# Decoder layer on one core: scan halves redistributed over the score slots, and the score stacks loaded by pairs of heads

## The chip, the cores and the metric

The kernel runs on one core of a Trainium2 chip. The metric is the device time of one execution in microseconds. Three executions of the kernel before took 1580.32, 1584.42 and 1585.39 us; their median is 1584.42 us. The profile is of a fourth execution.

## The reference

Four batches, each 512 rows of 512 values, go through one post-norm decoder layer of three blocks, each followed by a residual addition and a layer norm:

```python
x = layernorm(x + attention(x))          # 16 heads of 32, softmax, plus a small "splat" term
x = layernorm(x + ssm(ctx, z=x))         # in-projection, conv of 4 taps, silu, selective scan of 16 states
x = layernorm(x + ffn(x))                # ternary weights, silu(gate) * up, rms norm, down projection
```

Attention is softmax(q k' / sqrt(32)) v for each head; in the splat term the attention weights come from distances of q and k to 8 points per head. The scan block works on the context, not on x, until its last product (y * silu(z)), so it can run beside the attention. For each of 512 channels and 16 states it computes

```python
state = state * exp(delta * A[n]) + (delta * u) * B[n]     # over 512 time steps
y    += state * C[n]
```

## The kernel before, in words

**Order of the work.** All four batches are unrolled by hand: for batch b (0 to 3) an attention phase and an FFN phase follow one another, and each engine (PE, ACT, DVE, POOL, and SP as the queue of most DMAs) has its own program of the phase, joined by semaphores. An engine does its own list strictly in order.

**Scan halves.** The scan of a batch is cut into 32 halves (n, a): state n of 16, channel half a of 2 (256 of the 512 channels). Half number g = 2n + a costs:
- ACT: `exp_dA` (L571), two activations of 512 steps into the buffer dA[a]; it waits until scan g - 2 is done.
- DVE: `scan_half` (L858), a product (L866), the scan itself (L874) and a product (L877). It waits for row n of B and C (`BC`, loaded on SP, L333), for dA and, in a ring of three buffers ST, for the accumulation of half g - 3.
- POOL: a DMA (L471) that adds the result to YA in memory, issued one half later.

SP loads row n + 1 of B and C when it comes to half (n, 0) in its own list (`load_next_bc`, L354), after the product of half (n - 1, 1).

**Where the halves go.** `fill_halves` puts some between the projections that open the attention phase (the fill stage), `tile_halves` puts the first 16 halves of batches 1 to 3 into the FFN phase of the batch before, and `slot_halves(j, first)` (L261) puts the rest into the four score slots. It returns, for slot j, one list for each of the four steps kt (called c on DVE). It is read by SP, POOL, ACT and DVE alike. In batch 0 (`first`) slots 0 to 3 have 3, 3, 4 and 3 halves and three more follow behind the slots. In batches 1 to 3 the slots have:

| slot | step 0 | step 1 | step 2 | step 3 |
|---|---|---|---|---|
| 0 | - | - | - | (11,1) (12,0) |
| 1 | - | (12,1) | - | (13,0) (13,1) |
| 2 | - | (14,0) | - | (14,1) (15,0) |
| 3 | - | - | - | (15,1) |

**A score slot.** Slot j handles the four heads 4j to 4j + 3. Queries and keys, split into a high and a low part of reduced precision, are stored to memory (`qk_parts`) and come back as stacks QS[j % 2] and KS[j % 2] of 96 rows for four heads; `load_stack` (L339) issues six DMAs of 256 KB for them, all on one semaphore. Stacks 0 and 1 are loaded in the fill stage, behind the stores of the units u = 2 and u = 3, and the stores of the next units stand behind them in SP's list; stacks 2 and 3 are loaded when the scores of slot 0 and of slot 1 are done (step 3, ahead of that step's `load_next_bc`).
 - The row maxima of slot j + 1 are found during slot j: PE computes 16 tiles (`max_scores`, L1249, matmul L1264), four for each head, in two banks, and DVE reduces each (L930). Tile m goes to head m // 4; tile m waits for the maximum of tile m - 2. In slots 1 and 2 the steps 0, 1 and 2 take 4, 6 and 6 tiles. PE waits for the stack before tile 0 only.
 - The maxima go through PE and ACT into the bias row of the stack (`bias_row`, L622).
 - For each step kt PE computes the scores of four heads in two pairs (L1373), ACT takes their exponentials (L709), and PE multiplies those of the step before with the values and with ones (L1281).
 - After the slot ACT makes the inverse of the denominators (`inverse_start`, L642, its last instruction L647), and DVE normalises (`normalise`, L932, L936 to L940).

**The last slot.** In slot 3 there are no maxima left to find. It has the end of the splat term (`splat_normalise` L964, the numerators L1405 on PE, `add_splat` L983 on DVE, which frees their banks and on which the numerator two groups later waits), and, but for batch 3, the start of the next batch's scan block: transposes of the context (L1223), the in-projections (L1232), their copies on ACT (L584, L590, L591) and the convolution on DVE (`conv`, L879, three instructions at L885 for each of four channel tiles). Because two banks are needed for that, scores use one pair of banks (4 and 5) in slot 3 of batches 0 to 2: PE's next pair of scores waits for ACT's exponentials of the pair before. In batch 3 all four banks are there. On ACT the `exp_dA` of a step stand ahead of that step's exponentials (L693 ahead of L697). On DVE, step 3 has `add_splat(2)`, the convolution of three channel tiles, and half (15,1); then come normalise(3), add_splat(3), the fourth convolution, and the first layer norm. PE's output projection (L1416) does three of four groups of heads for two row tiles after the last values, and all the rest after add_splat(3).

## Time and profile before

| | us |
|---|---|
| median of 3 executions | 1584.42 |
| profiled execution, its own time | 1582.52 |
| its span, first to last instruction | 1580.8 |
| PE busy | 1226.0 |
| DVE busy | 1246.4 |
| ACT busy | 759.4 |
| POOL busy | 213.3 |

The attention phases, from the first maximum of slot 0 to the end of the output projection, take in batches 1 to 3 some 145 to 170 us each. The timeline of an engine gives the start of a group of equal instructions, their time together, and in brackets how long the engine had been idle before it and on whom it had waited. An x8 beside a matmul counts passes.

### The profile page before, as it was taken

The page shows a single profiled execution, that of the slowest core. Times are in us where ns is not written, and L with a number is a line of the kernel's source. Part 1 is how long each engine was busy: PE and PEld are TensorE (multiplying, and loading weights), DVE is VectorE, ACT ScalarE, POOL GpSimd, SP SyncE. Part 2 cuts the span into 40 slices and gives each one's busy share as a digit, 9 for nine tenths or more (in the row PEclk, how much of TensorE's full clock was granted, in tenths as well). Part 3 has the DMA queues.
Part 4 walks back from the last instruction along what each step waited for, and adds up shares of the span by engine and source line. Part 5 has one row for each costly group of instructions (what it writes and reads, how often), then busy time and mean ns, then how long its engine had stood idle before and what let it go on. Part 6 is the DMA issues. An engine that isn't in the chain of part 4 may idle for free.

```text
span 1580.8 us, 14027 instructions
## 1 busy us (share of the span) xinstructions
PE 1226.0 (78%) x4570; PEld 570.7 (36%) x4570; DVE 1246.4 (79%) x1485; ACT 759.4 (48%) x1110; POOL 213.3 (13%) x247
## 2 busy tenths in 40 slices
PE   4664746778688897778888886878888887788796
PEld 3332212223244442323344532323344532333453
DVE  5867978777989996885889995785889995877534
ACT  6775425435366632545466642545466633534232
POOL 1000221000111132100111132000111132001000
PEclk8756878779789898879889997789889998779798
DMA  6843794555439868451249776451248777462131
GB/s 196 272 161 109 168 222 118 115 118 111 101 82 234 211 171 215 94 140 34 62 118 238 184 194 178 94 144 30 62 120 237 183 182 182 92 150 41 36 105 66
DMA packets 112151, 220.15 MB, mean 139 GB/s; under 512 B 14048, under 2 KB 24800, under 8 KB 112080
## 3 DMA queue, kind: packets, MB, share of 16 engines
q1 hardware_dynamic: 92704, 151.24, 32.9%
q0 software_dynamic: 18432, 67.12, 21.9%
q10 hardware_dynamic: 944, 0.92, 0.2%
q8 instruction: 36, 0.59, 0.1%
q14 instruction: 35, 0.29, 0.1%
HBM read 122.37 MB, written 29.62 MB: 96 GB/s over the span
## 4 chain that ended last, share of the span: by engine, by line
DVE 39%; PE 28%; issue 10%; DMA 6%; ACT 3%; SPq 1%; POOL 1%; DVEq 0%; ACTq 0%; POOLq 0%
DVE ST L874 14%; DVE ST L866 6%; PE ps L1463 5%; PE ps L1264 5%; DVE MX L930 5%; PE ps L1281 4%; DMA KS<-qk_parts 3%; PE ps L1416 2%; DVE RD L1077 2%; DVE ST L877 2%; DVE QAK L1092 2%; PE ps L1373 2%; PE ps L1432 2%; PE ps L1345 2%; DVE BST L910 1%
## 5 line engine op out<-in xcount | busy, mean ns | idle before, releaser
L874 DVE TENSOR_TENSOR_SCAN ST<-dA,ST 128x1024 f32<-128x1024 f32 x128 | 311.8, 2436 | 8.8 <-ACT dA L577 6.0
L930 DVE TENSOR_REDUCE MX<-ps 128x1 f32<-128x512 f32 x256 | 165.3, 686 | 117.5 <-PE ps L1264 117.4
L1463 PE MATMUL ps<-V,GU 128*128 128x512 f16 x1024 | 243.3, 394 | 5.6 <-DVE V L1059 5.6
L471 POOL DMA_DIRECT2D YA<-ST x128 | 111.0, 867 | 1012.2 <-DVE ST L877 953.9
L1264 PE MATMUL ps<-KS,QS 96*128 96x512 f32 x256 | 134.1, 599 | 116.0 <-DVE MX L930 53.0
L577 ACT ACTIVATE dA<-DL,Aneg 128x511 f32<-128x511 f32 x256 | 168.9, 713 | 82.9 <-DVE ST L874 82.6
L709 ACT ACTIVATE PT<-ps 128x1024 f32<-128x1024 f32 x128 | 126.4, 1021 | 124.4 <-PE ps L1373 123.7
L1432 PE MATMUL ps<-WP,QS 128*128 128x512 f32 x512 | 145.8, 429 | 28.3 <-DMA WP<-proj_tiles 20.6
L877 DVE TENSOR_TENSOR ST<-ST,BC 128x1024 f32<-128x1024 f32 x128 | 159.4, 1246 | 4.4
L866 DVE TENSOR_TENSOR ST<-DU,BC 128x1024 f32<-128x1024 f32 x128 | 156.8, 1225 | 6.7 <-DMA BC<-bc_rows 6.5
L1463 PEld LDWEIGHTS ps<-V,GU 128*128 128x128 bf16 x1024 | 98.2, 101 | 139.2 <-issue 32.1
L1264 PEld LDWEIGHTS ps<-KS,QS 96*128 96x128 f32 x256 | 58.1, 243 | 212.5 <-DVE MX L930 109.9
L1345 PE MATMUL ps<-XA,W 128*128 128x512 f32 x256 | 121.9, 623 | 0.0
L1432 PEld LDWEIGHTS ps<-WP,QS 128*128 128x128 f32 x512 | 98.7, 198 | 63.8 <-issue 24.6
L1373 PE MATMUL ps<-QS,KS 97*128 97x512 f32 x256 | 95.3, 472 | 20.2 <-ACT PT L709 18.6
L757 ACT CAST QS<-QAK 128x512 fp32r<-128x512 f32 x64 | 39.5, 618 | 121.4 <-DVE QAK L1092 121.4
L1281 PE MATMUL ps<-PT,V 128*32 128x512 f32 x512 | 86.6, 755 | 9.5 <-ACT PT L709 9.5
L1092 DVE TENSOR_TENSOR QAK<-QAK,ps 128x512 f32<-128x512 f32 x64 | 43.7, 683 | 51.9 <-PE ps L1463 51.9
L1281 PE MATMUL ps<-PT,ones 128*32 128x512 f32 x512 | 79.1, 694 | 0.0
L1345 PEld LDWEIGHTS ps<-XA,W 128*128 128x128 f32 x256 | 51.0, 202 | 61.6 <-issue 59.1
L1373 PEld LDWEIGHTS ps<-QS,KS 97*128 97x128 f32 x256 | 50.4, 215 | 57.3 <-ACT PT L709 26.0
L1416 PE MATMUL ps<-W,XA 128*128 128x512 f32 x128 | 61.9, 642 | 10.8 <-DVE XA L987 10.8
(230 smaller groups left out, 1606.9 us busy)
## 6 DMA issues: line engine op xcount, KB each, us to landing
YA<-ST POOLq DMA_DIRECT2D x128, 512.0 KB, 7.3
BC<-bc_rows SPq DMA_DIRECT2D x64, 512.0 KB, 6.3
qk_parts<-PT SPq DMA_DIRECT2D x64, 256.0 KB, 6.3
GU<-gu_tiles SPq DMA_DIRECT2D x64, 256.0 KB, 9.1
WP<-proj_tiles SPq DMA_DIRECT2D x64, 256.0 KB, 6.7
QS<-qk_parts SPq DMA_DIRECT2D x48, 256.0 KB, 5.3
KS<-qk_parts SPq DMA_DIRECT2D x48, 256.0 KB, 5.9
ST<-in_L_ffn_w_gate_up_dram SPq DMA_DIRECT2D x16, 256.0 KB, 3.5
```

The costliest lines, as they stand in the source:

```text
L577: last = nc.scalar.activation(dA[:, a, e, 1:S], DL[:, 2 * a + e, 1:S], ACT.Exp, scale=Aneg[:, 2 * a + e, n:n + 1])
L709: nc.scalar.activation(PT[:, kt % 2, 2 * p:2 * p + 2, :], ps[:, bank:bank + 2, :], ACT.Exp, scale=SCALE).then_inc(s_exp, 1)
L866: nc.vector.tensor_tensor(ST[:, ring(bb, n, a), :, :], DU[:, 2 * a:2 * a + 2, :], BC[:, n % 2, 0:1, :].broadcast_to((P, 2, S)), ALU.mult). ...
L874: nc.vector.tensor_tensor_scan(flat, dA[:, a, :, :].rearrange("p e s -> p (e s)"), flat, 0.0, ALU.mult, ALU.add).then_inc(s_scan, 1)
L877: nc.vector.tensor_tensor(st, st, BC[:, n % 2, 1:2, :].broadcast_to((P, 2, S)), ALU.mult).then_inc(s_prod, 1)
L930: nc.vector.tensor_reduce(MX[:, j % 2, qt, h:h + 1], ps[:, n % 2, :], AX_X, ALU.max).then_inc(s_mx, 1)
L1264: mm(ps[:, n % 2, :], QS[i][0:3 * D, h, qt * P:(qt + 1) * P], KS[i][0:3 * D, h, :], start=True, stop=True).then_inc(s_xs, 1)
L1281: last = mm(ps[D * h:D * h + D, bank, :], w, PT[:, kt % 2, h, :], start=(kt == 0), stop=(kt == KT - 1), tile_position=(0, D * h))
L1345: last = mm(bank, W[:, z, k, j * P:(j + 1) * P], XA[:, k, :], start=(k == 0), stop=(k == KT - 1))
L1373: last = mm(ps[:, score_bank(b, j, h), :], KS[i][0:3 * D + 1, h, kt * P:(kt + 1) * P], QS[i][0:3 * D + 1, h, :], start=True, stop=True)
L1432: last = mm(ps[:, 4 + r, :], HL[:, 2 * z + t % 2, r * P:(r + 1) * P], WP[:, t % 2, :], start=(t == 0 and z == 0), stop=(t == NT - 1 and z ...
L1463: last = mm(ps[:, f % F_RING, :], GU[:, t % GU_RING, k, m * P:(m + 1) * P], XHL[:, z, k, :], start=(k == 0 and z == 0), stop=(k == KT - 1 ...
```

## The change

`slot_halves` returns other lists. In batches 1 to 3 slots 0, 1 and 2 have two halves each, both in step 3, and slot 3 has three: (14,1) and (15,0) in step 1, (15,1) in step 2. In batch 0 slots 0 to 2 stay, and slot 3 has its same three halves as two in step 1 and one in step 2, none in step 3. On DVE the convolution of the first two channel tiles moves from step 3 of slot 3 to step 2, behind add_splat(1) and ahead of that step's half. `load_stack` issues twelve DMAs of 128 KB in place of six of 256 KB: first six for heads 0 and 1, then six for heads 2 and 3, each pair with a semaphore of its own. PE waits for the first pair before tile 0 and for the second before tile 8.

```diff
-        s_stack = [sem(f"s_stack{i}") for i in range(2)]
+        s_stack = [[sem(f"s_stack{i}_{pair}") for pair in range(HG // 2)] for i in range(2)]
...
             rest = todo(first)[len(places(first)):]
-            upto = [len(rest) * share // 14 for share in (0, 3, 6, 9, 12, 14)] if first else (0, 2, 5, 8, 9, 9)
+            upto = [len(rest) * share // 14 for share in (0, 3, 6, 9, 12, 14)] if first else (0, 2, 4, 6, 9, 9)
             mine = rest[upto[j]:upto[j + 1]]
             if j == NG:
                 return [mine]
             if j < NG - 1:
                 third = len(mine) // 3
                 return [[], mine[:third], [], mine[third:]]
-            return [mine[len(mine) * c // KT:len(mine) * (c + 1) // KT] for c in range(KT)]
+            return [[], mine[:2], mine[2:3], mine[3:]]
...
-                for r, (zq, zk) in enumerate(((0, 0), (0, 1), (1, 0))):
-                    for z, dst, part in ((0, QS[i], zq), (1, KS[i], zk)):
-                        src = qk_parts[b, z, part, P * j:P * j + P, :].rearrange("(h p) s -> p h s", p=D)
-                        sp.dma_start(dst[D * r:D * r + D, :, :].bitcast(F32), src).then_inc(s_stack[i], 16)
+                for pair in range(HG // 2):
+                    first_row = P * j + 2 * D * pair
+                    for r, (zq, zk) in enumerate(((0, 0), (0, 1), (1, 0))):
+                        for z, dst, part in ((0, QS[i], zq), (1, KS[i], zk)):
+                            src = qk_parts[b, z, part, first_row:first_row + 2 * D, :].rearrange("(h p) s -> p h s", p=D)
+                            sp.dma_start(dst[D * r:D * r + D, 2 * pair:2 * pair + 2, :].bitcast(F32), src).then_inc(s_stack[i][pair], 16)
...
                             if c == 2:
                                 add_splat(b, 0)
                                 add_splat(b, 1)
+                                if not last:
+                                    conv(b + 1, 0)
+                                    conv(b + 1, 1)
                             if c == 3:
                                 add_splat(b, 2)
                                 if not last:
-                                    for e in range(KT - 1):
-                                        conv(b + 1, e)
+                                    conv(b + 1, 2)
...
             def max_scores(b, j, lo, hi):
                 i = j % 2
-                if lo == 0 and hi > 0:
-                    pe.wait_ge(s_stack[i], 96 * (2 * b + j // 2 + 1))
                 if lo == 0 and hi > 0 and j == 0:
                     pe.wait_ge(s_hi, 2 * NG * b + 4)
                 for m in range(lo, hi):
                     n = 16 * j + m
                     h, qt = m // KT, m % KT
+                    if m % (2 * KT) == 0:
+                        pe.wait_ge(s_stack[i][h // 2], 96 * (2 * b + j // 2 + 1))
```

## Rows read from the trace of the kernel before

**Rows 1.** The page, busy time of each engine.

```profile
PE 1226.0 (78%) x4570; PEld 570.7 (36%) x4570; DVE 1246.4 (79%) x1485; ACT 759.4 (48%) x1110; POOL 213.3 (13%) x247
```

**Rows 2.** The waits: who waited for whom, us in total, times, longest.

```profile
PE ps L1264 <- DMA KS<-qk_parts: 52.7, 8, 11.5
```

**Rows 3.** Timeline of DVE, slot 1 of batch 2.

```profile
1025.74 1.22 DVE L866 TENSOR_TENSOR ST<-DU,BC 128x1024 f32<-128x1024 f32 x1
...
1030.46 2.56 DVE L930 TENSOR_REDUCE MX<-ps 128x1 f32<-128x512 f32 x4
1034.83 1.29 DVE L930 TENSOR_REDUCE MX<-ps 128x1 f32<-128x512 f32 x2 [1.80 <-PE ps L1264]
```

**Rows 4.** Timeline of PE, slot 1 of batch 2.

```profile
1031.20 1.09 PE L1264 MATMUL ps<-KS,QS 96*128 96x512 f32 x2 [3.38 <-DVE MX L930]
```

**Rows 5.** Timeline of DVE, slot 3 of batch 2.

```profile
1082.74 0.69 DVE L972 SCALAR_TENSOR_TENSOR QAK<-X 128x512 f32<-128x512 f32 x1
1092.06 1.61 DVE L987 SCALAR_TENSOR_TENSOR XA<-ps,par,XA 128x512 f32<-128x512 f32 x2 [8.63 <-PE ps L1405]
1101.57 0.75 DVE L987 SCALAR_TENSOR_TENSOR XA<-ps,par,XA 128x512 f32<-128x512 f32 x1 [7.91 <-PE ps L1405]
1102.24 7.57 DVE L885 SCALAR_TENSOR_TENSOR W<-W,convw 128x511 f32<-128x511 f32 x9
...
1114.45 0.68 DVE L936 TENSOR_TENSOR X<-ps,RD 128x512 f32<-128x512 f32 x1
```

**Rows 6.** Timeline of ACT, slots 2 and 3 of batch 2.

```profile
1061.13 2.54 ACT L577 ACTIVATE dA<-DL,Aneg 128x511 f32<-128x511 f32 x4
...
1109.10 0.63 ACT L647 ACTIVATE RD<-RD 128x512 f32<-128x512 f32 x1
```

**Rows 7.** Timeline of PE, slot 3 of batch 2 and the output projection.

```profile
1083.26 0.97 PE L1373 MATMUL ps<-QS,KS 97*128 97x512 f32 x2 [2.04 <-ACT PT L709]
...
1108.33 5.42 PE L1416 MATMUL ps<-W,XA 128*128 128x512 f32 x12
1117.36 10.55 PE L1416 MATMUL ps<-W,XA 128*128 128x512 f32 x20 [3.61 <-DVE XA L987]
```

**Rows 8.** Timelines of DVE (first two) and PE, slot 3 of batch 3.

```profile
1432.74 0.69 DVE L972 SCALAR_TENSOR_TENSOR QAK<-X 128x512 f32<-128x512 f32 x1
...
1439.41 0.75 DVE L987 SCALAR_TENSOR_TENSOR XA<-ps,par,XA 128x512 f32<-128x512 f32 x1 [3.08 <-PE ps L1405]
...
1444.59 14.00 PE L1416 MATMUL ps<-W,XA 128*128 128x512 f32 x32
```

**Rows 9.** Stack 2 of batch 2: first and last issue on SP, then us to landing.

```profile
1004.94 0.32 SPq L352 DMA_DIRECT2D QS<-qk_parts  x1
...
1007.45 0.43 SPq L352 DMA_DIRECT2D KS<-qk_parts  x1
...
QS<-qk_parts SPq DMA_DIRECT2D x1, 256.0 KB, 3.1
...
KS<-qk_parts SPq DMA_DIRECT2D x1, 256.0 KB, 7.0
```

**Rows 10.** Timeline of DVE: first maxima behind stack 0, batches 1 to 3.

```profile
608.61 1.29 DVE L930 TENSOR_REDUCE MX<-ps 128x1 f32<-128x512 f32 x2 [2.62 <-PE ps L1264]
...
961.62 1.29 DVE L930 TENSOR_REDUCE MX<-ps 128x1 f32<-128x512 f32 x2 [5.04 <-PE ps L1264]
...
1314.69 1.29 DVE L930 TENSOR_REDUCE MX<-ps 128x1 f32<-128x512 f32 x2 [2.76 <-PE ps L1264]
```

**Rows 11.** The same behind stack 2, batches 0, 2 and 3.

```profile
288.75 1.29 DVE L930 TENSOR_REDUCE MX<-ps 128x1 f32<-128x512 f32 x2 [3.81 <-PE ps L1264]
...
1015.01 1.29 DVE L930 TENSOR_REDUCE MX<-ps 128x1 f32<-128x512 f32 x2 [2.25 <-PE ps L1264]
...
1365.31 1.29 DVE L930 TENSOR_REDUCE MX<-ps 128x1 f32<-128x512 f32 x2 [3.04 <-PE ps L1264]
```

**Rows 12.** Timeline of DVE, fill stage of batch 0.

```profile
221.54 1.23 DVE L866 TENSOR_TENSOR ST<-DU,BC 128x1024 f32<-128x1024 f32 x1 [6.53 <-DMA BC<-bc_rows]
```

## Prediction

> **What bounds the kernel now.** I read the page first, then the waits, then the timelines of DVE, PE, ACT and SP over the attention phases. The page shows no single bound: PE and DVE are each busy for 78 to 79% of the span [rows 1], so what counts is which of them waits for which, stage by stage. The waits say that PE stood still eight times, 52.7 us in all, before its first maximum tile because a stack had not landed [rows 2]. The timelines then show three patterns that repeat in the batches.
>
> First, slots 1 and 2 are bound by DVE. After the sixth tile of step 1 DVE does a scan half from 1025.74 to 1030.5, and PE, with two banks only, waits 3.38 us for the next maximum [rows 3, 4].
>
> Second, slot 3 is bound by PE and ACT handing each other one pair of score banks: PE waits 2.04 us for exponentials [rows 7], while DVE is idle for 8.63 and 7.91 us [rows 5]. The slot's end is bound by DVE again: nine convolutions and a half run from 1102.24 to 1114.45, although the inverse was ready at 1109.73 [rows 5, 6], and PE's output projection stands still for 3.61 us for them [rows 7].
>
> Third, DVE itself has nothing to do while a stack lands: 2.62, 5.04 and 2.76 us in the fill stage [rows 10], 3.81, 2.25 and 3.04 us at the start of slot 1 [rows 11], and batch 1 has the same 3.0 us there. Batch 0 waits in its fill stage for a row of B and C instead [rows 12].
>
> **Term 1: one half fewer in slots 1 and 2, batches 1 to 3 (six places).** A half is product, scan, product: 1030.46 - 1025.74 = 4.72 us of DVE. That is the upper bound of one place. Tiles 10 to 15 now end at 1036.12, that is 10.4 us after step 1's last tile, whose maximum ended at 1025.8 [rows 3]. Without the half, they take their 5.7 us from row 1030.46 to 1036.12, plus about 1.0 us, since PE must make the scores of its step ahead of tile 10 and no longer does so behind a half. That leaves 6.7 us and a gain of 3.7 us. The lower bound is PE's wait alone, 3.4 us [rows 4]. Everything behind (transposed maxima, scores, the two halves of step 3) keeps its distance. ACT's exp_dA for step 3 wait for scans two halves back, which are done a slot earlier. The row of B and C for a moved half is asked for one slot or more ahead of its use. Six times 3.7: **-22.2 us**.
>
> **Term 2: three halves and the split convolution in slot 3.** For DVE the new work fits: from 1083.43 the halves of step 1 take 2 x 4.72 us and end at 1092.9, against a numerator that came at 1092.06 [rows 5]. The price is on ACT, where the exp_dA stand ahead of the exponentials. Two of them are 2.54 us [rows 6], and PE's next pair of scores waits for just these exponentials [rows 7]; so everything behind in slot 3 comes 2.5 us later. The exp_dA of step 2 lies in ACT's own wait for scores and replaces the one of step 3: nothing, or 0.4 us if that cover is gone. Six convolutions (6 x 0.84 = 5.0 us) and the third half (4.7 us) then lie in DVE's second idle time, 7.9 us, and spill by under 2 us into the wait for the inverse.
> - Batches 1 and 2: the inverse comes at 1109.73 + 2.5 = 1112.3, and normalise and add_splat(3), 2.9 us, end at 1115.2. PE's first twelve projection passes end at 1113.75 + 2.5 = 1116.3, so PE is late next, not DVE: 1117.36 - 1116.3 = 1.1 us gained. The twenty passes behind the idle time took 0.53 us each, against 0.45 in the twelve ahead of it [rows 7] and 0.44 in batch 3, where none was idle [rows 8]: 20 x 0.09 = 1.8 us more. Together 2.8 us, twice. Bounds: a loss of 2.5 us if the longer wait at the slot's start slows PE as well; a gain of 3.6 + 1.8 us if ACT's delay were hidden.
> - Batch 0: one exp_dA more in step 1, 1.3 us. The wait of normalise behind the inverse, 1114.45 - 1109.73 = 4.7 us in batch 2 and alike there, becomes zero, and DVE's three halves behind the slots keep DVE the bound: 4.7 - 1.3 = 3.4 us gained.
> - Batch 3 has no next batch: PE has neither transposes nor in-projections, and DVE little idle time in this slot. From 1433.43 the two halves end at 1442.9; add_splat(0) and (1) come behind them, PE's third and fourth numerator (in order, ahead of the scores of step 3) wait for them until 1444.5, so that add_splat(2) has its numerator some 0.9 us later, at 1445.4, and not at 1439.4 [rows 8]. All of PE's list behind it moves by that. A loss of 6.0 us; bounds 5 and 9.5 (all of two halves).
>
> Sum of term 2: 2 x 2.8 + 3.4 - 6.0 = **-3.0 us**.
>
> **Term 3: stacks by pairs.** The six DMAs of stack 2 land from 1004.94 + 3.1 = 1008.0 to 1007.45 + 7.0 = 1014.45 [rows 9]: one each 1.28 us, in order. With half the bytes in each, six land one each 0.64 us from 1007.4 on: the first pair is there at 1010.6, 3.8 us earlier, and the issue of the sixth, at 1007.45, allows that. What DVE gains is the smaller of its wait and 3.8 us: 3.8 + 3.0 + 2.25 + 3.0 = 12.1 us at slot 1 [rows 11], and 2.6 + 3.8 + 2.8 = 9.2 us in the fill stage [rows 10]. In batch 0's fill stage DVE waits for B and C, which stands behind the stack in the queue [rows 12]: no gain. At slot 2 DVE is busy when stack 3 lands: nothing. Half-size DMAs are nowhere in this trace. The bounds of a DMA are 0.64 us (by bytes) and 1.28 us (by count); I take the first, since the DMAs land as evenly as a stream of bytes would. At 1.28 us the term is zero or, with what is queued behind, a loss (below).
>
> Six more issues of 0.43 to 0.47 us [rows 9] hold SP for 2.8 us per stack. Behind them stand stores of queries and keys, and B and C; all of these wait for the backlog of the stack's bytes anyway (the last stack DMA lands 7.0 us after its issue), so this costs nothing while the backlog is longer than 2.8 us. Were that cover gone, ACT's next unit in each fill stage would be late, up to 2.8 us in four batches. I put down a loss of 1.5 us in all. The second pair is wanted at tile 8, about 9 us behind tile 0 at slot 1, and lands no later than 3 us after the old stack. Term 3: **-19.8 us**.
>
> By the Trainium skill, page "DMA: Bandwidth & Descriptors", section "Rules for kernel authors", splitting a transfer into disjoint parts is not worth it, since both parts run on the same 16 engines and serialize, and DMAs should be large. What the rows show is that they do serialize, and that is what the early wait uses. By the Trainium skill's table of sizes (same page, section "Bandwidth"), an estimate for 128 KB is nearer 1 us than 0.64, so the first pair would gain 1.5 to 2 us rather than 3.8, and term 3 would be about half.
>
> **Sum.** -22.2 - 3.0 - 19.8 = -45.0 us. From the profiled execution's 1582.5 that is 1537.5. The median of the runs lies 1.9 us above that execution: **1539 us**.
>
> **The rivals.**
> - *The split loses its rate.* A half-size DMA takes as long as a whole one up to the point where the first pair lands as late as the stack did. For it: no such DMA in the trace. Against it: even landings. Term 3 is near zero: 1539 + 19.8 = 1559 us. Half-way, at 0.96 us each, 1549. The Trainium skill's rule above is this case.
> - *Slot 3 takes back more.* ACT's 2.5 us are paid, and PE runs slower behind the longer waits, so the projection's 1.8 us don't come: batches 1 and 2 lose 2.5 us each, batch 0 gains nothing, batch 3 pays 9.5 us. Term 2 becomes +14.5 in place of -3.0: 1556 us. For it: PE's 0.53 us passes. Against it: DVE's idle 16.5 us in two waits.
> - *Slower.* Each half-size DMA costs the full 1.28 us of the queue. Then a stack takes 7.7 us longer and what is queued behind it in the fill stage comes 7.7 us later: B and C in batch 0, where the 6.53 us [rows 12] become 14, and the stores on which ACT's next unit waits in the other three. That is 31 us on top of 1559: 1590 us. It decides from a spacing of about 1.2 us; at 1.0 us, the backlog costs less than half of that and the change still wins by term 1.
> - The change does what it says: the lists are fixed when the program is built.
>
> **How the numbers follow.** Forecast 0.68; the split loses its rate 0.13; slot 3 takes back more 0.15; slower 0.04. About 0.3% is what a measurement of this kernel can tell from no change: 4.8 us. All but the last lie beyond it: faster 0.96, same 0.01, slower 0.03. The range: below, term 1 at its upper bound (6 x 1.0 us more), both of batches 1 and 2 at theirs (2 x 2.6) and the 5.04 us wait gone entirely, 1.2: 1539 - 12.4, and some for PE's passes in the slots: 1524. Above it takes in slot 3's rival and the half-way case of the split, to 1557; left out are the full loss of the split and the slower case.
>
> **What would show it.** Slots 1 and 2: no L866 between the sixth and seventh maximum, and the maxima of step 2 ending 3.7 us earlier. Slot 3: DVE's waits before L987 nearly gone, ACT with four L577 ahead of step 1's exponentials, L936 directly behind L647, no wait before the twenty passes of L1416; in batch 3 a wait of PE for L987. Stacks: landings 0.64 us apart, DVE's waits of rows 10 and 11 near zero. Landings more than 1 us apart, or a new wait of ACT for qk_parts, would make term 3 wrong; a DVE wait in step 2 as long as the half was would make term 1 wrong.

## The result, and the profile after

The changed kernel takes **1520.3 us** (median of 4 runs, 1517.1 to 1522.4) against 1584.2 us before (4 runs beside it): a ratio of 0.9599, with a 95% interval of 0.9574 to 0.9624. That is 63.9 us less where 45 were forecast, and it lies 4 us below the range. The sign and the likeliest case were right; the size was not, and most of what follows asks where the other 19 us come from.

The page after, its first line and the busy times; and from the waits the three that matter (engine, line, who is waited for: us in total, how often, the longest). Lines 930, 1264, 1373, 987 and 936 of before are 932, 1268, 1377, 989 and 938 here.

```profile
span 1516.6 us, 14134 instructions
...
PE 1194.1 (79%) x4565; PEld 560.5 (37%) x4570; DVE 1245.1 (82%) x1485; ACT 759.7 (50%) x1110; POOL 214.6 (14%) x247
```

```profile
DVE MX L932 <- PE ps L1268: 84.0, 73, 3.8
...
PE ps L1377 <- ACT PT L711: 25.6, 14, 4.5
...
PE ps L1268 <- DMA KS<-qk_parts: 20.9, 4, 7.8
```

DVE does the same work as before, to 1.3 us [rows 1], in a shorter span. PE's wait for the stacks fell from 52.7 us [rows 2] to 20.9. But PE's *busy* time fell by 32 us too, although the two kernels make the same matmuls. No term of the prediction had anything of that kind. The mean granted clock of PE rose from 0.848 to 0.869 of full speed.

By stages, differences after minus before in the profiled executions (starts of instructions, read from the timelines; "fill" runs from the start of the span, or from PE's first feed-forward matmul of the batch ahead, L1463 and now L1467, to DVE's first maximum of the batch; slots 0 and 1 end at normalise(0) and normalise(1), slot 2 at the last instruction of `splat_normalise`, the last column at PE's first feed-forward matmul):

| batch | fill | slot 0 | slot 1 | slot 2 | slot 3 and projection |
|---|---|---|---|---|---|
| 0 | +0.2 | -4.0 | -0.1 | -5.0 | -3.1 |
| 1 | -1.4 | -3.2 | -4.5 | -6.5 | -1.5 |
| 2 | -6.0 | -6.4 | -4.2 | -6.3 | -1.8 |
| 3 | -3.4 | -3.6 | -4.6 | -5.6 | +7.1 |
| sum | -10.5 | -17.1 | -13.3 | -23.4 | +0.8 |
| forecast | -7.7 | -12.1 | -11.1 | -11.1 | -3.0 |

The start of slot 1, with its stack wait, counts in the column of slot 0, because normalise(0) stands behind it. The largest miss is slot 2: 12 us.

**Slot 1.** DVE's timeline of the changed kernel, batch 2 (start, us, engine, line, [idle before <- on whom]):

```profile
986.04 2.58 DVE L932 TENSOR_REDUCE MX<-ps 128x1 f32<-128x512 f32 x4 [1.55 <-PE ps L1268]
989.35 1.29 DVE L932 TENSOR_REDUCE MX<-ps 128x1 f32<-128x512 f32 x2 [0.73 <-PE ps L1268]
990.55 1.22 DVE L868 TENSOR_TENSOR ST<-DU,BC 128x1024 f32<-128x1024 f32 x1
```

The half is gone. In its place there are two short waits, 1.55 + 0.73 us, where the old slot had one of 1.80 [rows 3]: of the half's 4.7 us 0.5 were paid back, not the 1.0 I had put in.

**Slot 2.** The same stretch, tiles 8 to 15: first the kernel before, then the changed one.

```profile
1057.38 1.29 DVE L930 TENSOR_REDUCE MX<-ps 128x1 f32<-128x512 f32 x2 [0.96 <-PE ps L1264]
1058.59 1.22 DVE L866 TENSOR_TENSOR ST<-DU,BC 128x1024 f32<-128x1024 f32 x1
...
1063.31 1.28 DVE L930 TENSOR_REDUCE MX<-ps 128x1 f32<-128x512 f32 x2
1064.88 1.29 DVE L930 TENSOR_REDUCE MX<-ps 128x1 f32<-128x512 f32 x2 [0.29 <-PE ps L1264]
1068.07 1.29 DVE L930 TENSOR_REDUCE MX<-ps 128x1 f32<-128x512 f32 x2 [1.90 <-PE ps L1264]
```

```profile
1011.19 1.29 DVE L932 TENSOR_REDUCE MX<-ps 128x1 f32<-128x512 f32 x2 [1.77 <-PE ps L1268]
1013.69 2.58 DVE L932 TENSOR_REDUCE MX<-ps 128x1 f32<-128x512 f32 x4 [1.21 <-PE ps L1268]
1016.99 1.29 DVE L932 TENSOR_REDUCE MX<-ps 128x1 f32<-128x512 f32 x2 [0.72 <-PE ps L1268]
```

From the end of the first two maxima to the end of the last: 1069.36 - 1058.67 = 10.7 us before, 1018.28 - 1012.48 = 5.8 after. The waits are 0.29 + 1.90 before and 1.21 + 0.72 after, 0.26 us *less*: here the whole half, 4.7 us, was gain, and 0.2 more.

**Slot 3, batch 2.** ACT, PE and DVE of the changed kernel, one timeline each.

```profile
1030.36 2.56 ACT L579 ACTIVATE dA<-DL,Aneg 128x511 f32<-128x511 f32 x4
```

```profile
1033.88 1.22 PE L1377 MATMUL ps<-QS,KS 97*128 97x512 f32 x2 [4.47 <-ACT PT L711]
1035.03 1.94 PE L1285 MATMUL ps<-PT,V 128*32 128x512 f32 x8
1036.74 1.93 PE L1285 MATMUL ps<-PT,ones 128*32 128x512 f32 x8
1038.61 4.00 PE L1236 MATMUL ps<-QAK,inT 128*128 128x512 f32 x8
...
1059.84 14.00 PE L1420 MATMUL ps<-W,XA 128*128 128x512 f32 x32
```

```profile
1043.57 1.61 DVE L989 SCALAR_TENSOR_TENSOR XA<-ps,par,XA 128x512 f32<-128x512 f32 x2 [2.45 <-PE ps L1409]
...
1061.27 0.69 DVE L938 TENSOR_TENSOR X<-ps,RD 128x512 f32<-128x512 f32 x1 [3.42 <-ACT RD L649]
```

The pattern is the forecast one: two `exp_dA` of two activations each (the x4) ahead of the exponentials, PE's wait 4.47 us in place of 2.04 [rows 7] (2.4 more, 2.5 forecast), DVE's idle 16.5 us [rows 5] down to 2.45 before L989, the normalise behind the inverse, and 32 projection passes in one run at 0.44 us each. What I had not counted are the next PE rows. Behind the wait the two groups of eight take 1.94 and 1.93 us and L1236 takes 4.00, where later in the slot the same groups take 1.07, 1.04 and 3.70. The granted clock was at its lower level, 1.2 GHz (0.50 from 1034 to 1038 us, and 0.50 in the same stretch of batch 1). Before, behind the 2.04 us, the clock was low too (0.57 from 1083 to 1087 us) but came back sooner: scores, both groups and the in-projection took 0.97 + 1.93 + 1.59 + 3.70 = 8.2 us, now 1.22 + 1.94 + 1.93 + 4.00 = 9.1.

**Batch 3, slot 3.** PE, then DVE:

```profile
1373.01 3.03 PE L1409 MATMUL ps<-QAK 128*128 128x512 f32 x4 [4.56 <-DVE XA L989]
```

```profile
1382.46 0.69 DVE L938 TENSOR_TENSOR X<-ps,RD 128x512 f32<-128x512 f32 x1 [3.56 <-ACT RD L649]
```

As forecast, PE waits for a numerator that stands behind two halves: 7.1 us lost, 6.0 forecast.

**The stacks.** Issues of stack 2 in batch 1 on SP, the first, sixth and last of twelve; then from the view of DMA issues how long the sixth and the last took to land (us at the line's end):

```profile
634.76 0.32 SPq L354 DMA_DIRECT2D QS<-qk_parts  x1
...
637.32 0.43 SPq L354 DMA_DIRECT2D KS<-qk_parts  x1
...
640.63 1.39 SPq L354 DMA_DIRECT2D KS<-qk_parts  x1
```

```profile
KS<-qk_parts SPq DMA_DIRECT2D x1, 128.0 KB, 3.1
...
KS<-qk_parts SPq DMA_DIRECT2D x1, 128.0 KB, 5.8
```

The first pair is complete 637.32 + 3.1 - 634.76 = 5.7 us after the first issue: the forecast, 1010.6 - 1004.94. The second is complete 11.7 us after the first issue, some 2 us later than the whole stack before (9.5 us in [rows 9]; 9.9 for this stack in batch 1). The first eight halves land 0.4 to 1.1 us apart, 0.6 on average, where their issues stand 0.5 apart on average; the last four land 2.0, 1.2, 0.6 and 0.9 us apart.

### The profile page after: what moved, and what is told of

It reads as the page before. It is cut to its first block, busy times and chain, and to the rows that moved or that the text cites. A ratio compares the mean times of both kernels' runs of the same rounds, so it can differ in the third digit from the quotient of the medians.

```text
span 1516.6 us, 14134 instructions
## 1 busy us (share of the span) xinstructions
PE 1194.1 (79%) x4565; PEld 560.5 (37%) x4570; DVE 1245.1 (82%) x1485; ACT 759.7 (50%) x1110; POOL 214.6 (14%) x247
## 4 chain that ended last, share of the span: by engine, by line
DVE 39%; PE 30%; issue 10%; ACT 5%; DMA 4%; POOL 1%; SPq 1%; DVEq 0%; ACTq 0%; POOLq 0%
DVE ST L876 14%; DVE ST L868 6%; PE ps L1467 5%; PE ps L1285 5%; DVE MX L932 5%; PE ps L1268 4%; PE ps L1420 3%; PE ps L1349 2%; PE ps L1436 2%; DVE ST L879 2%; PE ps L1377 2%; DVE RD L1081 2%; DVE QAK L1096 2%; DMA qk_parts<-PT 2%; PE ps L1236 1%
## 5 line engine op out<-in xcount | busy, mean ns | idle before, releaser
L1467 PE MATMUL ps<-V,GU 128*128 128x512 f16 x1024 | 240.3, 390 | 5.6 <-DVE V L1063 5.6
L1268 PE MATMUL ps<-KS,QS 96*128 96x512 f32 x256 | 127.6, 560 | 74.1 <-DVE MX L932 42.3
L1467 PEld LDWEIGHTS ps<-V,GU 128*128 128x128 bf16 x1024 | 97.6, 100 | 136.5 <-issue 27.3
L1268 PEld LDWEIGHTS ps<-KS,QS 96*128 96x128 f32 x256 | 53.6, 223 | 164.7 <-DVE MX L932 95.1
L1285 PE MATMUL ps<-PT,V 128*32 128x512 f32 x512 | 81.1, 710 | 11.4 <-ACT PT L711 10.4
L1285 PE MATMUL ps<-PT,ones 128*32 128x512 f32 x512 | 74.6, 658 | 0.0
```

The lines of the kernel that those rows point to most:

```text
L1268: mm(ps[:, n % 2, :], QS[i][0:3 * D, h, qt * P:(qt + 1) * P], KS[i][0:3 * D, h, :], start=True, stop=True).then_inc(s_xs, 1)
L1285: last = mm(ps[D * h:D * h + D, bank, :], w, PT[:, kt % 2, h, :], start=(kt == 0), stop=(kt == KT - 1), tile_position=(0, D * h))
L1467: last = mm(ps[:, f % F_RING, :], GU[:, t % GU_RING, k, m * P:(m + 1) * P], XHL[:, z, k, :], start=(k == 0 and z == 0), stop=(k == KT - 1 ...
```

## What the rival theories were

*Theory C (the clock).* Each of these waits costs PE more than its length: the granted clock falls during it and what follows runs at half speed. Earlier stacks and fewer halves take these falls away; this is what the sum left out. *Rival W.* The waits are everything, and the sum was wrong because waits were sized too small (above all "the smaller of its wait and 3.8"). Windows of the timelines show what they argue about, around the start of slot 2 in batch 0: first before, then after. The columns are stretch, its length, busy us (and instructions) of PE, PEld, DVE, ACT and POOL, then the granted clock, DMA share, GB/s.

```profile
321.00:325.00 4.00, 1.15 (x4) 0.36 (x3) 1.43 (x2) 0.81 (x2) 0.00 (x0) 1.00 1.07 270
325.00:329.00 4.00, 3.45 (x9) 2.18 (x9) 2.77 (x5) 0.62 (x1) 0.00 (x0) 0.60 0.96 278
329.00:333.00 4.00, 4.00 (x14) 1.39 (x13) 2.38 (x4) 1.43 (x2) 0.00 (x0) 0.54 0.03 9
```

```profile
320.00:324.00 4.00, 3.72 (x18) 1.71 (x18) 3.98 (x7) 2.05 (x2) 0.00 (x0) 1.00 1.03 249
324.00:328.00 4.00, 3.78 (x24) 1.51 (x16) 3.23 (x5) 1.12 (x2) 0.00 (x0) 1.00 0.18 37
```

Before, PE waited for stack 3 while DVE had nothing to do either, and behind the wait PE's clock was 0.60, then 0.54 (the 1.2 GHz level is 0.50). After, it stayed at 1.00. In the prediction this wait stood as "DVE is busy when stack 3 lands: nothing". Two cautions go with these windows. The wait of before is longer here than this load needs: stack 3 took 11.6 us from its first issue to its last landing in this execution, and 9.8 in e2 below, which loads it whole too; there DVE waited 0.60 us in place of 2.56. And the windows are one execution of each kernel; e1 below shows the clock falling at this place with the stack early.

## The experiments

The variants were measured in three groups, each with runs of the kernel before beside it (medians 1581.2 for e1 to e4, 1581.2 for e7 to e10 and 1581.9 us for the others). A gain in us is one minus the ratio, times that median, unless medians are named. A ratio's interval is 0.0016 to 0.004 to either side, mostly 0.0025 or some 4 us; a difference of two ratios has an interval of some 5 to 6 us. By stages means one profiled execution of each kernel against one of before.

### The two parts alone

e1: the kernel before, with `load_stack`, `s_stack` and the waits of the change and nothing else of it.

```diff
-    for r, (zq, zk) in enumerate(...):  # six DMAs of 256 KB, one semaphore
+    for pair in range(HG // 2):         # twelve DMAs of 128 KB, one semaphore for each pair
...
+                    if m % (2 * KT) == 0:
+                        pe.wait_ge(s_stack[i][h // 2], 96 * (2 * b + j // 2 + 1))
```

> The kernel before with the stacks loaded by pairs, lists and convolution as before. Theory (PE's granted clock: a stall for a stack costs its own time and then a stretch in which PE runs at the lower level, so that removing the stall gains more than the stall, and stack 3 counts too): about 37 us faster than before, 1547 us, with slot 2 of batch 0 some 4 us shorter though nothing in it is moved. Rival 1 (the stalls are worth their length only, as predicted): 20 to 23 us, 1562 us. Rival 2 (the extra gain comes from the moved halves): 20 us here, and more than 40 us in the kernel with the lists alone.

Measured: 1551.1 us, ratio 0.9808 (0.9786 to 0.983): **-30.3 us**, where term 3 said -19.8: between the 20 to 23 us of one expectation and the 37 of the other.

e2: the changed kernel with stacks loaded as before, so lists of halves and convolution alone.

```diff
-        s_stack = [[sem(f"s_stack{i}_{pair}") for pair in range(HG // 2)] for i in range(2)]
+        s_stack = [sem(f"s_stack{i}") for i in range(2)]
```

> The kernel after with the stacks loaded whole, as before. Theory: 22 to 28 us faster than before (4.3 us for each of six places in slots 1 and 2, nothing to 3 us in slot 3), 1558 us. Rival 1: 25 us as predicted, 1559 us. Rival 2: over 40 us, 1543 us.

Measured: 1553.2 us, 0.9828 (0.9802 to 0.9855): **-27.2 us**, where terms 1 and 2 said -25.2. So the larger part of the miss is in term 3. The two ratios multiply to 0.9639 against 0.9599 for both together, 6 us with an uncertainty as large: whether the parts help each other stays open.

By stages e1 has -11.2 in the fill, -13.0 in slot 0, +0.4, -4.0 in slot 2, +0.6. e2 has -1.5, +1.0, -11.9, -19.7, +0.4. Of e2's slot 2, 16.8 us are in batches 1 to 3 and 2.9 in batch 0, whose list is unchanged there: in that slot this trace of before is itself at the slow end. So e1's 4.0 us in slot 2 are not the early stack's as they stand: 3.1 of them are in batch 0, where e2 has 2.9 with the stack late. In e1 the clock fell there all the same, with DVE's wait down to 0.59 us:

```profile
324.00:328.00 4.00, 4.00 (x14) 1.51 (x13) 2.58 (x4) 1.93 (x2) 0.00 (x0) 0.50 0.71 175
```

### The split without its early wait

e3: e1 with both pairs awaited before tile 0.

```diff
-                    if m % (2 * KT) == 0:
-                        pe.wait_ge(s_stack[i][h // 2], 96 * (2 * b + j // 2 + 1))
+                    if m == 0:
+                        for pair in range(HG // 2):
+                            pe.wait_ge(s_stack[i][pair], 96 * (2 * b + j // 2 + 1))
```

> The kernel before with twelve half-size DMAs per stack, but PE waits for both pairs ahead of tile 0. Tells whether the split itself costs or gives queue time. If half-size DMAs go by their bytes: within 3 us of before (1584 us). If each costs as much as a whole one: 25 to 31 us slower. If the split itself is what gains: faster by over 10 us.

Measured: 1602.7 us, 1.0131 (1.0091 to 1.0171): **21 us slower** than before, and between the two costs that were expected (within 3 us, or 25 to 31). The split costs something, and all of e1's gain is the early wait: 51 us lie between the two. The first and last issue of stack 3 in batch 1, the last one's landing, and what DVE then waited:

```profile
692.00 0.30 SPq L354 DMA_DIRECT2D QS<-qk_parts  x1
...
699.81 0.43 SPq L354 DMA_DIRECT2D KS<-qk_parts  x1
```

```profile
KS<-qk_parts SPq DMA_DIRECT2D x1, 128.0 KB, 5.9
```

```profile
706.75 1.29 DVE L932 TENSOR_REDUCE MX<-ps 128x1 f32<-128x512 f32 x2 [5.06 <-PE ps L1267]
```

The stack is complete 13.7 us after its first issue (10.3 before), and DVE's wait is 5.06 us where it was 1.07.

### The clock, with dummy matmuls

e4: before, with dummy matmuls of 128 x 256 in front of the waits for stacks 2 and 3 (six and three; the trace shows each as two passes). The waits stay, each stack's now directly ahead of its tile 0; PE is busy during them.

```diff
+                    if m == 0:
+                        for _ in range((0, 0, 6, 3)[j]):
+                            mm(ps[:, 0, 0:H // 2], W[:, 3, 0, 0:P], W[:, 3, 1, 0:H // 2], start=True, stop=True)
+                        pe.wait_ge(s_stack[i], 96 * (2 * b + j // 2 + 1))
```

> The kernel before, with PE doing matmuls that nobody reads (6 units of 256 columns ahead of tile 0 of stack 2, 3 ahead of tile 0 of stack 3, into the bank that tile 0 then overwrites) while it waits for the stack; all waits stay. Theory (clock): PE stays at its upper level behind the wait, and the first eight tiles of slots 1 and 2 take 7.2 us in place of 9.2: 5 to 12 us faster than before, 1575 us. Rival 1 (length of the stall only): no faster, 0 to 3 us slower.

Measured: 1571.1 us, 0.9938 (0.9914 to 0.9963): **-9.8 us** from matmuls that compute nothing. The window at the start of slot 2 in batch 0, and DVE there:

```profile
322.00:326.00 4.00, 3.26 (x12) 1.58 (x10) 3.71 (x6) 1.10 (x2) 0.00 (x0) 1.00 1.07 249
```

```profile
322.29 5.16 DVE L930 TENSOR_REDUCE MX<-ps 128x1 f32<-128x512 f32 x8 [1.89 <-PE ps L1266]
```

The wait for the stack is still there (1.89 us), but the eight maxima behind it run back to back, 5.2 us, at clock 1.00. Before, behind a wait of 2.56 us, they took from 325.35 to 331.80, 6.5 us, with three more waits among them, and the next two came 1.45 us later, where they come after 0.7 in e4. That is theory C's mechanism, with the stack no earlier. By stages slot 2 is 7.7 us shorter, 3.2 in batch 0 (where e2 has 2.9 with no dummies) and 1.9, 1.5 and 1.1 in the others; the profiled execution is the fastest of the nine, 6.5 us below their median.

e5: the same with 14 dummies, in front of stack 0 alone ((14, 0, 0, 0) in the line above).

> Before, with 14 dummy matmuls on TensorE in front of the wait for stack 0, which the 4.7 to 8 us wait of the next batch's first tile otherwise leaves idle. If what follows the stack waits is slow also because the granted clock has fallen during them, the tiles behind the wait get cheaper in the fill and in the first score slot: 1 to 2 us a batch, 3 to 8 us in all (time near 1576). If the clock plays no part there: nothing, or 1 to 3 us more, because the dummies end after the stack has landed.

Measured: 0.9998 (0.9981 to 1.0014): **nothing** in the whole, but not nothing in the trace. In batches 2 and 3 slot 0 is 4.5 and 3.4 us shorter while the fill keeps its length to 0.8 us. In batch 0 it is 8.1 us longer. One late window of slot 0 in batch 3, before and in e5 (DVE's wait for the maxima in it was 5.46 us before and 3.82 in e5):

```profile
1334.00:1339.00 5.00, 4.45 (x15) 1.15 (x11) 1.04 (x2) 1.50 (x4) 0.05 (x1) 0.78 0.05 18
```

```profile
1335.00:1340.00 5.00, 3.90 (x12) 1.92 (x12) 4.24 (x7) 4.16 (x7) 3.34 (x3) 1.00 0.01 3
```

And half of what batch 0 of e5 lost, in PE's timeline; before, this wait was 3.13 us:

```profile
296.47 1.19 PE L1266 MATMUL ps<-KS,QS 96*128 96x512 f32 x2 [6.98 <-DMA KS<-qk_parts]
```

The clock and slot 0's length go together in this trace too, but my expectation that it would show in the time fell. e5 also moves the waits for all stacks as e4 does, so that move is not what made e4 faster. Stack 2 of batch 0 landed later here; whether the dummies caused that or it varies between executions was not settled. Batch 0's slot 0 differs by -0.7 to +3.4 us in e1 and e2.

Slot 0's clock also varies with nothing changed. In batch 1 the kernel of e10 (below) runs the same instructions as the changed kernel, and in its trace slot 0 is 3.6 us longer: the clock was 1.00 there in the changed kernel, and in e10

```profile
624.00:629.00 5.00, 4.64 (x12) 3.04 (x12) 3.56 (x7) 3.14 (x5) 3.11 (x3) 0.61 0.30 58
```

and a group of eight took 1.94 us in place of 1.07. A difference of this size in one slot of one trace does not show what an edit did.

e11: the *changed* kernel with dummies in front of four of its waits.

```diff
+                    if j == 0 and m == 0:   # 8 dummies, stack 0
+                    if j == 2 and m == 2:   # 3 dummies, behind a wait for s_exp
...
+                                if one_pair and kt == 1 and p == 1:   # 8 dummies, last slot's second score pair
...
+                                pe.wait_ge(s_br, NG * b + 3)          # and 3 dummies, in slot 2
```

> The changed kernel with dummy matmuls in front of four of its waits: 8 ahead of the first tile of stack 0, 3 ahead of tile 2 of slot 1, 3 ahead of the normalise wait of slot 2, 8 ahead of the second score pair of step 1 in the last slot of batches 0 to 2. The theory (a wait also costs the clock of the matmuls behind it) says that the change has taken away part of these falls, and what is left is worth 5 to 10 us: near 1512. The rival (the clock is a remainder, the waits themselves are everything): within 3 us of the changed kernel, and slower where a dummy ends after what it waits for.

Measured: 1507.4 us, 0.9537 (0.9518 to 0.9556). Against the changed kernel's ratio, 0.0062 or **9.8 us less** (by some 5 us to either side), at the upper end of what was expected; the mean clock is 0.890. The place where it comes from is mostly the last slot: -5.3, -5.4 and -3.9 us in batches 0 to 2, where the change alone has -3.1, -1.5 and -1.8. PE there in batch 1, first the changed kernel, then e11:

```profile
702.79 1.22 PE L1377 MATMUL ps<-QS,KS 97*128 97x512 f32 x2 [4.47 <-ACT PT L711]
703.94 1.94 PE L1285 MATMUL ps<-PT,V 128*32 128x512 f32 x8
```

```profile
701.38 0.73 PE L1387 MATMUL ps<-QS,KS 97*128 97x512 f32 x2 [1.02 <-ACT PT L711]
702.04 1.06 PE L1292 MATMUL ps<-PT,V 128*32 128x512 f32 x8
```

### The last slot

e7: the changed kernel with the three convolutions together again in step 3.

```diff
-                                if not last:
-                                    conv(b + 1, 0)
-                                    conv(b + 1, 1)
...
-                                    conv(b + 1, 2)
+                                    for e in range(KT - 1):
+                                        conv(b + 1, e)
```

> The kernel after with nine convolution instructions in step 3 of the last slot, none in step 2, as before. Theory: the end of the slot is set by PE and ACT now, and DVE's step 3 has 3.4 us of idle time behind it in batches 0 to 2, so the split is worth 0 to 1 us per batch: 0 to 3 us slower than after. Rival (DVE still sets the end of the slot): 5.0 us per batch, 15 us slower.

Measured: 1520.3 us, 0.9622 (0.9591 to 0.9653), with slot 3 within 0.2 us of the changed kernel's in every batch. Splitting the convolution brings nothing that shows: the normalise waits for ACT's inverse in both.

e8: the changed kernel, but batch 3 with the old upper bounds (0, 2, 5, 8, 9, 9) and its one half of slot 3 in step 3.

```diff
+            if b == B - 1:
+                return [[], [], [], mine]
```

> The kernel after with the lists of before for batch 3 alone. Theory: slot 3 of batch 3 gets back its 7.1 us, slots 1 and 2 lose 4.5 and 5 us: 2 us slower than after. Rival (the moved halves are paid for in full wherever there is no idle time, so that batch 3 gained nothing from them): 5 us faster or more.

Measured: 1522.8 us, 0.9635 (0.961 to 0.966): 2.4 us slower than the changed kernel by the medians, 5.7 by the ratios, which is at the edge of the interval. By stages, batch 3's slots 1 and 2 give back 3.7 and 5.3 us (9.0 together) and slot 3 gets 7.1. So by the trace the last batch earns its halves' move after all, by 1.9 us; the times do not contradict it.

e9: the changed kernel with the first of the last slot's `exp_dA` pairs issued one step earlier, ahead of the inverse of slot 2 and the exponentials of step 0.

```diff
+                    if j == NG - 1:
+                        exp_dA(b, *halves[1][0])
...
-                        for n, a in halves[kt]:
+                        for n, a in halves[kt][1 if j == NG - 1 and kt == 1 else 0:]:
```

> The kernel after; ACT does the first exp_dA of step 1 of slot 3 ahead of inverse_start, where it waits 2 us for PE anyway. Theory (ACT's exp_dA ahead of the exponentials are on PE's path): 1.3 us in each of batches 0 to 2, and up to 1 us more each if PE's granted clock stays up: 4 to 7 us faster than after. Rival (ACT's delay is hidden): no change.

Measured: 1511.9 us, 0.9567 (0.954 to 0.9595): **5 us** less by the ratios, 8 by the medians; 5 is within the interval of a difference, and the case rests on the trace, here and in e13. Slot 3 gains 1.9, 3.7 and 3.7 us more in batches 0 to 2, for 1.3 us of ACT moved. PE in batch 2:

```profile
1027.10 1.22 PE L1379 MATMUL ps<-QS,KS 97*128 97x512 f32 x2 [3.25 <-ACT PT L713]
```

The wait is 1.2 us shorter than the changed kernel's 4.47, and the second group of eight behind it is back at 1.21 us, where the changed kernel's took 1.93.

e10: the changed kernel with batch 3's three halves in steps 1, 2 and 3, one each.

```diff
+            if b == B - 1:
+                return [[], mine[:1], mine[1:2], mine[2:]]
```

> The kernel after; in batch 3 the last slot has one half in each of steps 1, 2 and 3 in place of two and one. Theory (batch 3 loses 7 us because add_splat(0) and (1), on which PE's third numerator waits, stand behind two halves): PE's wait of 4.6 us there becomes about 0 and the slot 3 us shorter, 3 us faster than after. Rival (DVE's three halves are too much for the slot in any order): no change.

Measured: 1516.2 us, 0.959 (0.9564 to 0.9615). Slot 3 of batch 3 loses 2.6 us in place of 7.1. That is 4.5 us in the trace and 4.2 in the medians, inside the interval of the ratios. PE no longer waits for the second numerator, and what is left is a wait before the projection's last passes:

```profile
1387.39 4.99 PE L1422 MATMUL ps<-W,XA 128*128 128x512 f32 x11 [1.52 <-DVE XA L991]
```

### A version that beats both

e13 is e9 and e10 together; e12 is e13 with the dummies of e11 (six in place of eight in the last slot).

> The two edits of the last slot together: one half of the exponentials goes ahead of step 1's, and in the last batch the halves are spread over the steps and one is left behind them. Alone they measured 8.4 and 4.2 us below the changed kernel's median; they touch different batches but for the last, so the sum is 9 to 12 us: 1508 to 1511. A rival: in the last batch the two edits meet on ScalarE and give back 3 us: 1512 to 1514.

> Both edits of the last slot and the dummy matmuls. If the dummies' gain is of the clock and not of the order of the work, it adds to the 9 to 12 us of the two edits: 5 to 10 us more, near 1502. If the edits of the last slot took away the same waits at which the dummies help, only the ones in the fill and in slots 1 and 2 are left: near 1507.

Measured: e13 1512.3 us, 0.9558 (0.9537 to 0.958); e12 **1501.6 us**, 0.9494 (0.9474 to 0.9515). e13's slot 3 has both gains in its trace (-12.0 us in all against before, where e9 has -8.5, e10 -4.0 and the change alone +0.8). By the ratios it is 0.0041 or 6.5 us below the changed kernel and by the medians 8, short of the 9 to 12 expected; its median is no lower than e9's. The dummies add 0.0064, 10 us, as they did without the two edits. e12 is 80 us below the kernel before, and 17 below the change by the ratios.

## Why the prediction was right, and where it failed

**Term 1 (-22.2)** was too small by 6 to 9 us: e2 has 11.9 us in slot 1 and 16.8 in slot 2, 28.7 in all; the changed kernel has 31.6, some of it the stacks'. The mechanism held. The step that failed is "plus about 1.0 us, since PE must make the scores of its step ahead of tile 10", taken from slot 1 for both. It measured 0.5 us in slot 1, and in slot 2 a gain of 0.3. I had computed a place at 3.7 us once and multiplied it by six. The slots differ, and rows of slot 2 were in the trace. Of the rest of slot 2, 0.7 us a place in e2, a wait of DVE for ACT behind the normalise explains 0.6 in batch 2 (0.57 us at L968 before, gone after); for batches 1 and 3 the rest was not traced.

**Term 2 (-3.0)** came out at about +0.6 (+0.8 after, +0.4 in e2). Batch 0 got 3.1 to 3.4 (3.4 forecast), batches 1 and 2 got 1.5 and 1.8 in place of 2.8 each, batch 3 paid 7.1 in place of 6.0. ACT's 2.5 us, PE's waiting and the projection's rate were right. The step that failed is the price of the longer wait: I put down its length alone, while the scores and the three groups behind it took 0.9 us more (9.1 against 8.2), most of the 1.0 to 1.3 us by which batches 1 and 2 fell short. I had named it as a bound ("if the longer wait at the slot's start slows PE as well") and did not put it into the sum. e11 and e9 show what waits and slow rows of this place still cost together: 1.9 to 4.0 us a batch. The convolution's split, to which I gave a place in DVE's idle time, has no price either way (e7).

**Term 3 (-19.8)** measured -30.3 alone (e1). Two of its steps failed. The landing of the first pair was forecast to 0.1 us (5.7 us behind the first issue), with some luck: the first half landed 0.3 us later than forecast and the six stood 0.56 us apart, not 0.64. In the other batches' stacks 2 and 3 it took 5.9 to 6.8 us. The step "at slot 2 DVE is busy when stack 3 lands: nothing" was wrong: DVE waited 2.56 us there in batch 0 (and 1.1, 1.8 and 0.7 in the others), and the clock fell behind it. In batches 1 to 3 this is worth 0.8 us in all in e1, and 4.5 in e4; batch 0's 3.1 and 3.2 us are mostly its own variation, as e2's 2.9 show. The step "what DVE gains is the smaller of its wait and 3.8" was wrong in batch 2, where the 5.04 us [rows 10] went wholly, and where slot 0 gained 6.0 us in e1 for a wait of 2.25 [rows 11]. The difference goes with slot 0's clock: it stood at 0.66 and 0.70 late in that slot, and at 1.00 after:

```profile
981.00:986.00 5.00, 4.86 (x14) 1.04 (x10) 0.34 (x1) 1.18 (x3) 0.00 (x0) 0.66 0.14 54
986.00:991.00 5.00, 4.24 (x10) 2.72 (x11) 3.60 (x7) 3.20 (x5) 3.32 (x3) 0.70 0.13 25
```

```profile
946.00:951.00 5.00, 4.35 (x19) 1.28 (x16) 1.58 (x3) 2.63 (x6) 1.86 (x2) 1.00 0.30 113
951.00:956.00 5.00, 4.51 (x16) 2.53 (x15) 4.44 (x8) 4.16 (x7) 2.74 (x3) 1.00 0.38 73
```

That the early stacks caused this is not shown: e2, with the stacks late, has 2.4 us of it, e10 has the same fall of the clock in batch 1 with the stacks early, for 3.6 us, and this trace of before may simply have had it in batch 2. In batch 0's slot 0 e1 gained 0.7 us of the 3.8 forecast and the changed kernel 4.0. The 1.5 us loss for SP's six more issues did not show: slot 1 of e1 is within 0.4 us, and its fill gained 11.2 us, not less than the forecast's 7.7. It would show, and is much larger, where one waits for all twelve (e3).

**The rivals.** "The split loses its rate" fell as far as the first pair goes, which is what the early wait needs; for the whole stack it is true (e3). "Slot 3 takes back more" was true in kind: term 2 ended above zero, 3.8 us worse than forecast, of the 17.5 it allowed. "Slower" did not happen: ACT's waits for `qk_parts` grew only from 63.5 to 72.1 us in all (longest 13.6 and 12.9). The range failed on its lower side: it allowed 6.0 us more for term 1, which was 6.5 short, and only 1.2 more for term 3, which was 10 short. It had nothing in it for what waits do to PE's rate.

**What is settled and what is not.** C and W are both part of it. e4 shows that the slow clock behind the stack waits of before cost 9.8 us (6 to 14) that dummies could take back with the stacks no earlier; e3 against e1 shows that the whole gain of the split is its early wait. The miss of 19 us divides by terms: some 6.5 us are term 1's (the size of a place), 10 are term 3's beyond its sum, and -3.6 are term 2's; what is left, 6 us, is either joint gain or scatter. How much of term 3's 10 us is the clock's stays open. No run holds the clock fixed with the stacks early, and the slots of the trace that seemed to price it (slot 2 of batch 0, slot 0 of batch 2) vary by as much between executions.

The Trainium skill, page "DMA: Bandwidth & Descriptors", section "Rules for kernel authors", advises against two transfers to disjoint partition halves in place of one, since they share the same 16 engines and serialize. The split here is by heads, not by partition halves; the prediction carried the rule over. Taken so, e3 agrees (21 us slower) and e1 does not (30 us faster): the rule has no word on a reader that can start with the first part. The prediction's estimate from that page's table of sizes, that the first pair gains 1.5 to 2 us, was itself generous: a straight line between the table's 0.95 us at 64 KB and 6.15 at 1 MB gives an estimate of 1.3 us for 128 KB, and no gain. The traces decide: the pair landed 3.8 to 4.2 us earlier (5.7 us behind the first issue against 9.5 to 9.9).

The Trainium skill's page "TensorE: Matmul & The Clock Gate", section "Part 1: The HAM clock gate (the "warmup" mystery)", puts the penalty of the clock's ramp at under 1% of a typical kernel span. It says so of the ramp from a cold start, which no run here prices. The falls behind waits in mid-kernel are another matter: what dummies took back is 0.6% in e4 and 0.6% in e11, and that is not all that they cost, since the mean granted clock is still 0.869 of full speed in the profiled execution of e4 and 0.890 in that of e11.

## What to carry to other kernels

Where a change makes a wait of PE longer or shorter, look at the granted clock in the windows behind the wait and at the same group's duration early and late (1.94 against 1.07 us here): the price of a wait is its length and what runs slow behind it, and a longer wait put in on purpose pays both. Before a slot's difference between two traces is called the edit's, look for the same slot in a kernel that does not touch it (3.6 us between two traces of the same instructions here). Splitting a load pays only with a wait on the first part; the same split awaited whole cost 21 us. And a gain read in one slot is read again in the next before it is multiplied.

## What the runs showed of the hardware

Half-size DMAs (128 KB) on one queue were issued some 0.47 us apart, and six of them had landed 5.7 to 6.8 us after the first issue, where six of 256 KB took 9.3 to 11.6. Twelve of them took 11.6 to 13.7 us, longer than six whole ones of the same bytes in the same place; two of the later issues took 0.92 and 1.39 us in place of 0.43. A group of 8 matmul passes took 1.94 us behind a wait of 4.47 us, and 1.06 where dummies had filled all but 1.02 us of that wait. A dummy matmul of 128 x 256 is two passes of some 0.25 us at full clock (three dummies in 1.56 us). In e4's windows at the start of slot 2 of batch 0 the clock stood at 1.00 behind them, where it had been 0.60 and 0.54. In time dummies were worth 9.8 us in the kernel before (e4), 9.8 in the changed one (e11), and nothing in the place of e5. The same instructions at the same place took 3.6 us longer in one execution than in another, with the clock at 0.61 in place of 1.00 (e10 and the changed kernel, slot 0 of batch 1).
